# A vision-tower block on one core: both row biases added by GpSimd instead of TensorE, the power table in sixteen chunks, the small loads issued first, and new instruction lists

## The reference, cut to what matters

```python
h = s4d_kernel(log_dt, C=x, B, inv_A_real, A_imag, 1024)       # (64, 128, 1024): 2 Re(sum_n Cc[n] exp(dtA[n] * l))
h = concatenate([broadcast(cls_tok), h], axis=1)               # (64, 129, 1024): 64 steps, 129 rows

x = layernorm(h)                                               # attention part
d = gelu(transpose(x @ w_down.T + b_down))                     # 128 features
a = hydra(hydra(d))                                            # in-projection, causal conv of 7 taps, silu, scans both ways, gate, norm, out-projection
a = d + alpha * d + (1 - alpha) * a
h = h + x + transpose(a @ w_up.T + b_up)                       # b_up: one bias of 1024

x = layernorm(h)                                               # feed-forward part
base = x @ base_W.T + base_b                                   # base_b: the other bias of 1024
w = weights of the 8 experts from top_k(softmax(x @ router_W.T + router_b))
h = h + base + (((x @ A.T) * w) @ B) * 2
```

## Time and profile before

| what | us |
|---|---|
| median of 3 runs (2155.73 to 2158.18) | 2155.79 |
| the profiled execution: its own time | 2158.75 |
| its span, first to last instruction | 2157.0 |
| before iteration 0 | 37.2 |
| iterations 8 to 15 | 242.6 |
| iterations 16 to 61 | 1394.0 |
| iterations 62 to 69 | 231.2 |

### The profile page before, as it was taken

How to read it: one execution, slowest core, us unless ns; L and a number is a source line. 1 busy time by engine, 2 the same in 40 slices (tenths; PEclk the granted TensorE clock), 3 DMA queues, 4 the chain that set the end, 5 groups by cost and what they waited for, 6 DMA issues and landing times.

```text
span 2157.0 us, 53463 instructions
## 1 busy us (share of the span) xinstructions
PE 2078.5 (96%) x14483; PEld 1880.1 (87%) x14483; DVE 1766.7 (82%) x5078; ACT 1502.1 (70%) x3068; POOL 974.1 (45%) x1351
## 2 busy tenths in 40 slices
PE   3889999999999999999999999999999999999998
PEld 2677889999999999999999999999999999999887
DVE  5778988888888888888888888888888888878763
ACT  3787777677777777677777777677777777677652
POOL 3464644454444544444444544454444544444320
PEclk9999999999999999999999999999999999999998
DMA  4211312222122211222122211222122211222111
GB/s 126 80 59 38 90 40 65 68 68 64 39 68 68 68 42 61 68 68 67 35 68 68 68 40 62 68 68 67 36 68 68 68 44 58 68 69 62 54 34 36
DMA packets 90192, 132.65 MB, mean 61 GB/s; under 512 B 20507, under 2 KB 63687, under 8 KB 90134
## 3 DMA queue, kind: packets, MB, share of 16 engines
q1 hardware_dynamic: 89414, 129.33, 20.1%
q10 hardware_dynamic: 720, 2.62, 0.3%
HBM read 55.03 MB, written 76.74 MB: 61 GB/s over the span
## 4 chain that ended last, share of the span: by engine, by line
PE 54%; issue 20%; POOL 6%; ACT 3%; DVE 3%; POOLq 1%; DVEq 0%; ACTq 0%
PE bank L1766 20%; PE bank L1873 5%; PE bXYZ L1947 3%; PE bXYZ L1931 3%; POOL CB L923 3%; PE bank L1861 3%; PE bank L1827 2%; PE bXYZ L1959 2%; PE bank L1799 2%; ACT L1071 2%; PE bXYZ L1907 1%; POOL XD L874 1%; PE bXYZ L1978 1%; PE bXYZ L1889 1%; PE bank L1801 1%
## 5 line engine op out<-in xcount | busy, mean ns | idle before, releaser
L1766 PE MATMUL bank<-w_hi,XHI 128*128 128x392 f32 (+1 forms) x1560 | 599.5, 384 | 0.0
L1766 PE MATMUL bank<-w_lo,XHI 128*128 128x392 f32 (+1 forms) x1560 | 529.0, 339 | 0.0
L1766 PE MATMUL bank<-w_hi,XLO 128*128 128x392 f32 (+1 forms) x1560 | 528.3, 339 | 0.0
L1284 DVE SCALAR_TENSOR_TENSOR CX<-bXYZ,cw,CX 128x252 f32<-128x252 f32 (+5 forms) x804 | 343.5, 464 | 55.1 <-ACT CX L1009 55.0
L1766 PEld LDWEIGHTS bank<-w_hi,XHI 128*128 128x128 f32 x1560 | 295.5, 189 | 13.7
L1766 PEld LDWEIGHTS bank<-w_lo,XHI 128*128 128x128 f32 x1560 | 295.6, 189 | 9.1
L973 ACT ACTIVATE T<-bank 64x512 f32<-64x512 f32 x256 | 151.5, 592 | 214.2 <-PE bank L1861 209.5
L1766 PEld LDWEIGHTS bank<-w_hi,XLO 128*128 128x128 f32 x1560 | 293.8, 188 | 0.0
L923 POOL TENSOR_TENSOR CB<-CB,CM 128x126 f32<-128x126 f32 (+5 forms) x402 | 170.2, 423 | 167.2 <-ACT CM L973 137.7
L887 POOL TENSOR_TENSOR lone<-lone 128x1 f32<-128x1 f32 x65 | 35.3, 543 | 374.2 <-DVE lone L1476 374.2
L914 POOL TENSOR_TENSOR RB<-m_gt,AS 128x512 fp32r<-128x512 f32 x134 | 156.4, 1169 | 85.4 <-DVE AS L1550 85.4
(11 more groups left out here) (293 smaller groups left out, 5449.3 us busy)
## 6 DMA issues: line engine op xcount, KB each, us to landing
carried<-T SPq DMA_DIRECT2D x65, 512.0 KB, 4.6
T<-carried SPq DMA_DIRECT2D x65, 512.0 KB, 3.8
out<-HB SPq DMA_DIRECT2D x129, 256.0 KB, 3.2
tables<-tab SPq DMA_DIRECT2D x8, 560.0 KB, 4.0
TB<-tables SPq DMA_DIRECT2D x62, 70.0 KB, 2.7
carried<-U SPq DMA_DIRECT2D x65, 64.0 KB, 3.5
XM<-carried SPq DMA_DIRECT2D x65, 64.0 KB, 4.6
XI<-in_x SPq DMA_DIRECT2D x128, 32.0 KB, 2.7
```

What stands on the lines that cost most here:

```text
L1284: inc(STT(CX[:, c, :, s:CS], src[:, :, 0:CS - s], cw[:, c, k:k + 1], CX[:, c, :, s:CS], ALU.mult, ALU.add), "conv")
L1766: ins = mm(bank[:, 0:c1 - c0], xs_[:, 1 - p, k, :], ws[:, k, c0:c1], start=(c0 == C2 and k == 0 and n == 0), stop=(c0 == C2 and k == KC - ...
```

## The change

- The tiles `biases`, `up_sel` and `base_sel` go, and the five bias matmuls of an iteration with them. The first matmul of each group now starts the accumulation.
- Two tiles `up_rows` and `base_rows` hold each bias on all 128 partitions. GpSimd gets two steps: `carry_bias` adds `up_rows` to T after `carry_h`, so that the residual brings `b_up` along, and `base_bias` adds `base_rows` to HB ahead of `final` and `add_base`. SyncE's store of T now waits for two steps on T, and `final` and `add_base` wait for `base_bias`.
- `HCH` is 8: sixteen chunks of half the size, the first before iteration 0 and one in each of the iterations 0 to 14.
- In the first block the ten small loads are issued ahead of those of `lora_B`, and the bias rows go last under a semaphore of their own; on GpSimd the products of the first chunk come after the one-hot table.
- The written-out iterations are 0 to 15, the loop is 16 to 61. Each engine has four lists: iterations 0 to 7, 8 to 14, 15 with the loop, and from 62 on.
- `warm` multiplies `ident` by itself (128 columns) instead of `biases` (512 columns).

```diff
-        up_sel = sb("up_sel", [P, P], F32R)
-        base_sel = sb("base_sel", [P, P], F32R)
-        biases = sb("biases", [P, HID], F32R)
+        up_rows = sb("up_rows", [P, HID])
+        base_rows = sb("base_rows", [P, HID])
...
-        HCH = 16
+        HCH = 8
...
-                small(bias_s[UP_ROWS, :], b_up.unsqueeze(0).broadcast_to([64, HID]))
-                small(bias_s[BASE_ROWS, :], base_b.unsqueeze(0).broadcast_to([64, HID]))
...
-                n = pieces.index(("b", 0))
-                st4 = stage[n].rearrange("p (a e r) -> p a e r", a=KC, e=NE)
-                for e in range(NE):
-                    sp.dma_start(st4[:, :, e, :], lora_B[e].rearrange("(a p) r -> p a r", p=P)).then_inc(s_ld[n], 16)
                 sp.wait_ge(s_zero, 3)
...
+                n = pieces.index(("b", 0))
+                st4 = stage[n].rearrange("p (a e r) -> p a e r", a=KC, e=NE)
+                for e in range(NE):
+                    sp.dma_start(st4[:, :, e, :], lora_B[e].rearrange("(a p) r -> p a r", p=P)).then_inc(s_ld[n], 16)
+                for rows, src in ((up_rows, b_up), (base_rows, base_b)):
+                    sp.dma_start(rows[:, :], src.unsqueeze(0).broadcast_to([P, HID])).then_inc(s_rows, 16)
...
-        LOOP_FROM, LOOP_TO, LAST = 8, CLS - 2, TILES + 5
+        LOOP_FROM, LOOP_TO, LAST = 16, CLS - 2, TILES + 5
...
-                        wait(sp, i, tt=1)
+                        wait(sp, i, tt=2)
...
+                    def carry_bias():
+                        if A1:
+                            wait(pool, i, tt=1)
+                            if isinstance(i, int) and i == 0:
+                                pool.wait_ge(s_rows, 32)
+                            inc(pool.tensor_tensor(T[:, p, :], T[:, p, :], up_rows[:, :], ALU.add), "tt")
+
+                    def base_bias():
+
+                        if E:
+                            wait(pool, te, xh2=1)
+                            inc(pool.tensor_tensor(HB[:, 1 - p, :], HB[:, 1 - p, :], base_rows[:, :], ALU.add), "hb")
...
-                            wait(dve, te, o=h + 1)
+                            wait(dve, te, o=h + 1, hb=1)
...
-                            wait(dve, te, rt=1)
+                            wait(dve, te, rt=1, hb=1)
...
-                                mm(bO[1][:, :], up_sel[:, :], biases[:, 0:512], start=True, stop=True)
+                                mm(bO[1][:, 0:P], ident[:, :], ident[:, :], start=True, stop=True)
...
-                            if a == 0:
-                                mm(bR[:, 0:HC], base_sel[:, :], biases[:, C2:HID], start=False, stop=False)
...
-                                mm(bO[h][:, 0:C1], base_sel[:, :], biases[:, C1 * h:C1 * (h + 1)], start=True, stop=False)
...
-                            mm(bU[:, :], up_sel[:, :], biases[:, c], start=True, stop=False)
```

More of the change, by code:

```diff
@@ L1639, in body @@
                         conv(5, 1)
                         conv(6, 0)
-                        final(0)
-                        conv(6, 1)
+                        weighted_lo()
+                        table_values()
+                        conv(6, 1)
+                        split_decays(0)
+                        split_decays(1)
+                        split_lo(0)
+                        decays_forth(0)
+                        decays_forth(1)
+                        final(0)
+                        final(1)
```

734 lines of the change are left out of this document (546 added, 188 removed).

## The result

The changed kernel takes 2216.41 us (median of 4 runs, 2215.79 to 2220.68) against 2156.98 of the kernel before on the same chip: a ratio of 1.0277, interval 1.0261 to 1.0294, **2.8% slower**. The prediction was 2159 with a range of 2106 to 2186. The profiled execution of after took 2215.99 for a span of 2214.3, 57.3 more than the span of before.

The account below looks back on a forecast made before the run. TensorE was taken to bound the old loop; VectorE and GpSimd's round would bound the new one. Loop +19, start -5.5, prologue -4 - 1, tail -5 gave +3.5 us, on the median 2159 us, range 2106 to 2186.

Parts of the forecast that it names:

- The loop: Iterations of the main loop: 30.7 us each instead of 30.30, +0.4, so +19 us over 47.
- The chain: From AS (VectorE's second split_decays) to Mt, two-operand SBUF work of VectorE and GpSimd runs serially: 12.0 us instead of 10.6.
- rival B: Loop, slower: the 1024-wide add takes 2.38 us, the round 31.2 to 31.4, total 2185 us; chance 0.22.
- Each 0.1 us is 4.7 us: Loop: from an add of 2.2 us on, each further 0.1 us of add costs 4.7 us in total.
- rival A: Loop, faster: carry_bias hides under VectorE's PSUM work, TensorE stays the bound, 2096 to 2121 us; chance 0.35 with Rival C.
- Iterations 8 to 14: Eight table chunks, 2 us of VectorE each, mostly in its waits, with a shorter seam: -1 us (-7 to +8).
- the seam: VectorE and GpSimd between two iterations; shorter in 8 to 14, as carry_h and carry_bias stand ahead of both RB.
- What leaves TensorE: Five bias matmuls per iteration go, 0.93 us; were TensorE still the bound, an iteration would take 29.37 us.
- Rival C: Loop: the rows leave TensorE, a 0.93 us wait replaces them, 30.3 per round, total 2140; chance 0.35 with rival A.
- Start: Before iteration 0: earlier small loads and no bias splits on GpSimd, -5.5 us (-3 to -7).
- Tail: Iterations 62 to 69: no tables, less VectorE work, at most eight times 0.93 gained; -5 us (-7.5 to 0).
- Wrong if: Signs against: loop iteration at or under 30.0, adds over 2.3 us, or iterations 8 to 14 over 1 us slower than the loop.

Follow-up runs that it names:

- e15: The changed kernel with carry_bias on the first 512 of 1024 columns only, so half of T gets no b_up: 2155.2 us.
- e3: The changed kernel with neither carry_bias nor base_bias, so no bias is added anywhere: 2149.1 us.
- e1: The changed kernel without carry_bias, all lists kept: 2149.6 us.
- e2: The changed kernel without base_bias, all lists kept: 2212.9 us.
- e14: The changed kernel with GpSimd's table products and both RB ahead of carry_h and carry_bias in iterations 8 to 14: 2228.3 us.
- e6: The changed kernel with carry_bias of the tile before put behind base_bias, and T stored an iteration later: 2283.7 us.
- e8: The changed kernel with the last eight of twelve convolution steps on VectorE writing 8 steps of time only: 2207.4 us.
- e4: The kernel before without its five bias matmuls per iteration and nothing in their place: 2140.8 us.
- e11: The kernel before with the eight loads of lora_B issued behind the last small loads: 2158.0 us.
- e18: The kernel before with small loads first, one-hot map ahead of products, bias splits on VectorE, and new lists from iteration 62, rows kept: 2151.7 us.

## Why the prediction was wrong, step by step

**The loop: mechanism right, size off.** Forecast +0.4 per iteration and +19 us for 47; measured +0.73 and +34.5. The chain is the one worked out, at the places named (TensorE at turn_x, VectorE at gram_sum, Mt 12.2 after AS). The term that was mis-sized is the add: 2.14, "since V has all 128 partitions", where 2.35 to 2.39 is measured alone and 2.69 in its place; and Mt to AS was 18.79 for 18.6, worked out from 19.52 in one short iteration (30.14; the mean of that piece is 19.76). The rest of the difference is rival B, whose price was 2.38 and whose round was 31.2 to 31.4 (measured 31.02). "Each 0.1 us is 4.7 us" can't hold down to small adds: half the add costs 0.05 in place of 0.91 (e15). A cover of the kind that rival A needed was there, but of some 1.3 us, GpSimd's wait for GB, half the add.

**Iterations 8 to 14: the step that failed.** Forecast -1 (-7 to +8), measured +33.7. The prediction put the chunk's work into VectorE's waits, so it cost nothing, and took the seam to be shorter. The seam is shorter, 9.83 for 10.58; the work is not free. The runs give for the 33.7: 20.7 without any add (e3 against before: 233.1 to 212.4), 10.5 from carry_bias (e1) and 2.8 from base_bias (e2), 34.0 together, some 1.5 of it through the clock. The 20.7 are 3.0 per iteration, the new work on VectorE is 2.6 (forecast 2), and VectorE's idle time did not shrink (4.9 us, before 4.5): the work came on top of the waits. The 10.5 of carry_bias came by the cast to AS, which the prediction did not have: the add held it for 1.8 us, and Mt to AS is 24.49 with the add and 22.85 without (e1). Freeing the cast moved the price into the seam (e14); behind base_bias the add cost nothing (e6). This miss alone carries the time out of the range: with the loop as measured and -1 here it would be 2182. Open is why the round grows by the work. Chunks and lists of these iterations were not tried apart, and e8, where VectorE had 2.0 us less to do in each, was only 0.2 faster there at the same clock, so the sum of VectorE's work alone does not set them. (There are seven chunks in these iterations; the prediction counted eight.)

**What leaves TensorE.** The 0.93 per iteration was worth 0.18 of the loop (e4). The forecast bounded the loop from below at 29.37; without the rows and without adds it stood at 30.12 to 30.16 (e4, e1, e3). Rival C, counted with A, had the mechanism, a wait in place of the rows.

**Iterations 2 to 7.** The prediction's -4 stood for 0 to 7; 2 to 7 came at +5.0. Without the adds they are 4.2 shorter (e3), as forecast; the adds cost some 9, which were left out.

**Start.** Forecast -5.5, measured -6.1 at iteration 2. The sum was right, in part by luck. TensorE's first transposes of iteration 0 begin at 29.67 instead of 37.24, in the forecast 5.5 to 7.9 earlier. Of this 1.5 is lost again by iteration 2, as forecast, but to carry_bias: without it iteration 2 begins at 80.0 (e1) and not at 81.9. And the ground, that the loads are 7.1 earlier, was not enough: alone they bring 0.6 (e11).

**Tail.** Forecast -5, measured -9.7 in one profile, of which up to 4.6 may be the spread of that stage: before had the lowest clock there, and against the two profiles of the old list at 0.98 (228.2 and 226.6), after's own, it is -5.1 to -6.7. Without rows the old lists came 7.5 lower (e4), and with the rows the new lists 3.8 (e18): the forecast had the rows alone.

**base_bias costs nothing:** right in the loop (0.00), wrong in 8 to 14 (0.40 each), where the scaling of XM, on SBUF, stands beside it (1.18 us for 0.28).

Two of the three signs under "Wrong if" came true: adds over 2.3, and iterations 8 to 14 slower than the loop by more than 1 us.
